# Cross attention and FP4 feed-forward on one core: two TensorE products taken from fp32 operands to pairs of fp16 parts, with one scale for the whole context of a batch element

## The reference, cut to what matters

```python
def xattn(inp_q, ctx, ctx, Wt, Wp, Wg, Wz, gamma, beta):      # inp_q = layernorm(x)
    t = einsum('oc,bcd->bod', Wt, ctx)
    p = einsum('oc,bcd->bod', Wp, inp_q)
    g = einsum('oc,bcd->bod', Wg, ctx)
    att = einsum('bgcd,bgcd->bg', pg, gg) * 0.125             # one score for each of 8 groups of 32 channels
    u = einsum('goc,bgcd->bgod', Wz, att * tg)
    xn = groupnorm(u) * gamma + beta
    return xn + ctx
x = x + xattn(layernorm(x), ctx, ctx, ...)
gate, up = fp4(layernorm(x)) @ fp4(w_gate).T, fp4(layernorm(x)) @ fp4(w_up).T
x = x + fp4(silu(gate) * up) @ fp4(w_down).T                  # 512 -> 1408 -> 512
```

## Time and profile before

| what | before |
|---|---|
| median of 3 runs | 1733.88 us (1733.24 to 1734.05) |
| the profiled execution | 1733.28 us, of which the span of the profile is 1731.4 us |
| TensorE matmuls busy | 1677.1 us, 97% of the span |
| VectorE busy | 1501.5 us, 87% |
| ScalarE busy | 825.9 us, 48% |
| GpSimd busy | 722.5 us, 42% |
| mean granted TensorE clock | 0.998 of full speed |

### The profile page before, as it was taken

The page is one execution under the profiler, slowest core; times in us unless marked ns, Lnnn a source line. Parts: engine busy times, 40 slices in busy tenths (PEclk is TensorE's granted clock), DMA queues, the critical chain, the costliest instruction groups (busy, mean ns, idle before and its releaser), DMA issues.

```text
span 1731.4 us, 27880 instructions
## 1 busy us (share of the span) xinstructions
PE 1677.1 (97%) x8723; PEld 922.2 (53%) x8723; DVE 1501.5 (87%) x2577; ACT 825.9 (48%) x1472; POOL 722.5 (42%) x951
## 2 busy tenths in 40 slices
PE   2799999999999999999999999999999999999999
PEld 1665555555555555555555555555555555555544
DVE  7877888889888888988888898888888988888887
ACT  3665544544445444444545444454544445445422
POOL 7986343334444333444433334443333444433310
PEclk9999999999999999999999999999999999999999
DMA  8123334343434344343334434333434444343322
GB/s 258 34 43 81 83 91 95 88 100 89 95 81 94 89 91 99 88 106 76 88 89 100 94 85 104 76 89 91 103 88 94 95 82 92 91 94 88 76 50 49
DMA packets 412150, 155.86 MB, mean 90 GB/s; under 512 B 383200, under 2 KB 384480, under 8 KB 412128
## 3 DMA queue, kind: packets, MB, share of 16 engines
q1 hardware_dynamic: 396352, 125.17, 33.9%
q10 hardware_dynamic: 15776, 30.41, 5.5%
HBM read 43.03 MB, written 16.78 MB: 35 GB/s over the span
## 4 chain that ended last, share of the span: by engine, by line
PE 91%; POOL 6%; DVE 1%; DMA 1%; issue 1%; ACT 0%; SPq 0%; POOLq 0%; DVEq 0%; ACTq 0%
PE pairs L550 52%; PE work L561 26%; PE work L500 5%; PE work L512 3%; PE work L527 2%; PE ubank L527 2%; POOL raw L1864 2%; POOL raw L1853 1%; POOL w_parts L1864 1%; POOL w_parts L1853 1%; DMA raw<-in_L_ffn_w_gate 0%; DMA hT_parts<-raw 0%; POOL xc L1787 0%; PE pairs L580 0%; POOL q_parts L1803 0%
## 5 line engine op out<-in xcount | busy, mean ns | idle before, releaser
L550 PE MATMUL pairs<-w_gate_hi,xT_parts 128*128 128x512 f16 (+1 forms) x1536 | 555.1, 361 | 0.5 <-DMA xT_parts<-raw 0.5
L550 PE MATMUL pairs<-w_up_hi,xT_parts 128*128 128x512 f16 (+1 forms) x1536 | 554.7, 361 | 0.0
L561 PE MATMUL work<-w_parts,hT_parts 128*128 128x512 f16 x2079 | 458.9, 379 | 0.9 <-DMA hT_parts<-raw 0.9
L561 PEld LDWEIGHTS work<-w_parts,hT_parts 128*128 128x128 f16 x2079 | 203.5, 99 | 236.0 <-issue 1.1
L550 PE MATMUL pairs<-w_up_lo,xT_parts 128*128 128x512 f16 (+1 forms) x768 | 277.5, 361 | 0.0
L550 PE MATMUL pairs<-w_gate_lo,xT_parts 128*128 128x512 f16 (+1 forms) x768 | 277.4, 361 | 0.0
L550 PEld LDWEIGHTS pairs<-w_gate_hi,xT_parts 128*128 128x128 f16 x1536 | 152.7, 99 | 155.7 <-issue 8.2
L550 PEld LDWEIGHTS pairs<-w_up_hi,xT_parts 128*128 128x128 f16 x1536 | 150.3, 98 | 146.8
L964 ACT ACTIVATE early<-pairs,w_unit 128x512 f32<-128x512 f32 (+1 forms) x192 | 124.8, 650 | 163.2 <-PE pairs L550 163.2
L915 ACT ACTIVATE wm<-h 128x1408 bf16<-128x1408 f32 (+2 forms) x65 | 87.2, 1341 | 204.9 <-DVE h L1184 204.9
L873 ACT CAST raw<-hq 128x704 f16<-128x704 f32 x126 | 98.2, 779 | 180.0 <-DVE hq L1201 179.3
(11 more groups left out here) (193 smaller groups left out, 2801.7 us busy)
## 6 DMA issues: line engine op xcount, KB each, us to landing
out<-raw SPq DMA_DIRECT2D x64, 256.0 KB, 2.1
c_in<-in_ctx ACTq DMA_DIRECT2D x29, 512.0 KB, 3.8
x_in<-in_x ACTq DMA_DIRECT2D x29, 512.0 KB, 5.2
raw<-in_L_ffn_w_down SPq DMA_DIRECT2D x2, 1408.0 KB, 8.8
raw<-in_L_ffn_w_gate SPq DMA_DIRECT2D x2, 1280.0 KB, 8.5
w_parts<-in_L_ffn_w_up SPq DMA_DIRECT2D x2, 1280.0 KB, 9.2
x_in<-in_x SPq DMA_DIRECT2D x3, 512.0 KB, 4.1
c_in<-in_ctx SPq DMA_DIRECT2D x3, 512.0 KB, 4.7
```

The costliest lines, as they stand in the source:

```text
L550: mm = pe.matmul(pairs[:, pair, n, 0:b - a], xT[s][part][:, k, :], w1[n][wpart][:, k, a:b], start=(k == 0 and part == 0 and wpart == 0), s ...
L561: mm = pe.matmul(obank[:, :], hT[part][:, k, :], w2[wpart][:, k, :], start=(k == 0 and part == 0 and wpart == 0), stop=(k == KH - 1 and pa ...
```

## The change

`mixed` and `u_rows` take pairs of fp16 parts. For that the context of an element gets one power-of-two scale for all its 256 rows in place of one for each row, so that the scale can be taken out after the products; both weight matrices get one scale each. The same scaled fp16 parts `c_parts` that `turn_c` turns are now read by `u_rows` as well.

- **TensorE.** `mixed` issues 12 fp16 matmuls of 256 columns in place of 4 fp32 ones; `u_rows` issues its 12 matmuls of 512 columns from fp16 parts. `mixed` waits for `gram_lo`.
- **ScalarE.** `gram_copy` is one instruction that writes the high fp16 part. `ctx_hi` and `ctx_fit_lo` go (4 instructions of a 128x512 tile). `ctx_fit` writes the fp16 part and the scaled fp32 context, 4 instructions, and now stands behind `affine(i+1,0)`. Two DMAs are issued: `save_rows` writes the 256 sums of squares to DRAM after `ctx_square`, and `spread_rows` reads them back to all partitions, behind `silu_group(j,0,0)` and ahead of `copy_u`.
- **VectorE.** New are `gram_lo` (one instruction of 128x512, behind `normalise2`), `ctx_peak` (a maximum over 256 numbers, behind `gated(j,0,1)`) and `scale_of_u` (2 numbers). `ctx_power` moves from ahead of `gated(j,0,0)` to behind `gated(j,0,2)`, with `scale_of_u` behind it.
- **GpSimd.** `ctx_root` waits for `ctx_peak` and stands behind `columns`. Both `ctx_lo` stand behind `columns_affine`; each subtracts the fp16 part from the scaled fp32 context and waits for both outputs of `ctx_fit` of its tile.
- **The opening.** For element 0 the maximum over the partitions goes over TensorE (`attention_peak`, `attention_rows`, `attention_top`, `attention_spread`, `attention_parts`), together with the maxima of the two weight matrices; `attention_hi` and `attention_lo` make their fp16 parts. Elements 1 and 2 use the DRAM path.

```diff
@@ tensor
             def mixed(b):
-                pe.wait_ge(gram_copied, HT * b + HT)
+                pe.wait_ge(gram_lo_done, b + 1)
                 at_least(pe, pg_summed, HT * b)
                 dst = mixed_bank(b)
                 for s in range(HT):
                     for k in range(HT):
-                        mm = pe.matmul(dst[:, s * C:(s + 1) * C], wgT[:, k, s * P:(s + 1) * P], gram_sb[:, k, :],
-                                       start=(k == 0), stop=(k == HT - 1))
+                        for wpart, part in PARTS:
+                            mm = pe.matmul(dst[:, s * C:(s + 1) * C], wgT[wpart][:, k, s * P:(s + 1) * P], gram_sb[part][:, k, :],
...
-                        mm = pe.matmul(u_bank(b, s), wuT[wpart][:, k, s * P:(s + 1) * P], c_wide[part][:, k, :],
+                        mm = pe.matmul(u_bank(b, s), wuT[wpart][:, k, s * P:(s + 1) * P], c_parts[:, k, part, :],
...
+            def attention_rows():
+                pe.wait_ge(wu_peaked, 2)
+                pe.wait_ge(c_squared, HT)
+                for n, column in enumerate((wu_pow[:, 0, 0:1], wu_pow[:, 0, 1:2], c_norm[:, 0, 0:1], c_norm[:, 0, 1:2])):
+                    mm = pe.matmul(mixed_bank(0)[0:1, n * P:(n + 1) * P], column, ident[:, :], start=True, stop=True)
...
@@ scalar
+            def save_rows(b):
+                act.wait_ge(c_squared, HT * b + HT)
+                at_least(act, c_rows_spread, 16 * (b - 1))
+                nc.scalar.dma_start(c_rows, c_norm[:, 0, :]).then_inc(c_rows_saved, 16)
+            def spread_rows(b):
+                act.wait_ge(c_rows_saved, 16 * b)
+                at_least(act, c_peaked, b)
+                nc.scalar.dma_start(c_all[:], c_rows.rearrange("p h -> (p h)").unsqueeze(0).to_broadcast([P, HT * P])
...
             def ctx_fit(b):
...
                 for s in range(HT):
                     nc.scalar.activation(c_parts[:, s, 0, :], c_in[:, s, :], ACT.Identity,
-                                         scale=c_norm[:, 2, s:s + 1]).then_inc(c_fit_done, 1)
+                                         scale=c_norm[:, 2, 0:1]).then_inc(c_fit_done, 1)
+                    nc.scalar.activation(c_scaled[:, s, :], c_in[:, s, :], ACT.Identity,
+                                         scale=c_norm[:, 2, 0:1]).then_inc(c_scaled_done, 1)
...
@@ scalar, body(i)
                 silu_group(j, 0, 0)
+                if ahead:
+                    spread_rows(i + 2)
                 if more:
                     copy_u(i + 1, 0)
                     copy_u(i + 1, 1)
...
+                silu_group(j, 0, 1)
+                x_hi(j + 1)
+                silu_group(j, 0, 2)
+                if more:
+                    affine(i + 1, 0)
                 if ahead:
                     ctx_fit(i + 2)
-                silu_group(j, 0, 1)
-                x_hi(j + 1)
-                if ahead:
-                    ctx_hi(i + 2)
-                silu_group(j, 0, 2)
-                if more:
-                    affine(i + 1, 0)
-                if ahead:
-                    ctx_fit_lo(i + 2)
                 grain_h(j)
@@ vector
+            def gram_lo(b):
+                dve.wait_ge(gram_copied, b + 1)
+                nc.vector.scalar_tensor_tensor(out=gram_sb[1][:].rearrange("p h n -> p (h n)"), in0=gram_bank(b)[:, 0:HT * C],
+                                               scalar=SS, in1=gram_sb[0][:].rearrange("p h n -> p (h n)"), op0=ALU.mult,
+                                               op1=ALU.subtract).then_inc(gram_lo_done, 1)
...
@@ vector, body(i)
                 normalise2(j + 1)
+                if more:
+                    gram_lo(i + 1)
                 h_snap_add(j - 1)
...
                     ln1_moments(i + 2, 0)
-                    ctx_power(i + 2)
                 gated(j, 0, 0)
...
                 gated(j, 0, 1)
                 if ahead:
+                    ctx_peak(i + 2)
                     ln1_moments(i + 2, 1)
...
                 gated(j, 0, 2)
+                if ahead:
+                    ctx_power(i + 2)
+                    scale_of_u(i + 2)
                 h_first(j)
@@ gpsimd
             def ctx_lo(b, s):
-                pool.wait_ge(c_hi_done, HT * b + s + 1)
-                nc.gpsimd.tensor_tensor(c_wide[1][:, s, :], c_in[:, s, :], c_wide[0][:, s, :].bitcast(F32),
-                                        ALU.subtract).then_inc(c_ready, 1)
+                pool.wait_ge(c_fit_done, HT * b + s + 1)
+                pool.wait_ge(c_scaled_done, HT * b + s + 1)
+                nc.gpsimd.tensor_tensor(c_parts[:, s, 1, :], c_scaled[:, s, :], c_parts[:, s, 0, :],
+                                        ALU.subtract).then_inc(c_fit_ready, 1)
...
@@ gpsimd, body(i)
+                columns(i + 1)
                 if ahead:
                     ctx_root(i + 2)
-                columns(i + 1)
+                columns_affine(i + 1)
                 if ahead:
                     ctx_lo(i + 2, 0)
-                columns_affine(i + 1)
-                if ahead:
                     ctx_lo(i + 2, 1)
                     add_ctx(i + 2, 0)
@@ the opening, vector
             normalise1(0, 0)
-            attention_lo()
+            attention_peak()
             weight_top(0)
+            attention_top()
             weight_max(1, 0)
             normalise1(0, 1)
             weight_unit(0)
+            ctx_peak(0)
+            weight_max(1, 1)
             ctx_power(0)
-            weight_max(1, 1)
+            attention_parts()
+            scale_of_u(0)
             weight_round(0)
+            attention_lo()
...
             copy_group(0)
+            ctx_peak(1)
             ctx_power(1)
```

More of the change, by code:

```diff
@@ L39 @@
 QS = 2.0 ** 10
+SS = 2.0 ** -10
 def at_least(eng, sem, n):
@@ L958, in weight_grain, with attention_hi @@
                 grain(wm[n % 2], staged(m, c * H, H), w_y_done, n + 1, w_grain_done)
+            def attention_hi():
+                act.wait_ge(wu_steps, 6)
+                for n, (full, parts) in enumerate(((wu_full, wuT), (wg_full, wgT))):
+                    nc.scalar.activation(parts[0][:, :, :].rearrange("p a b -> p (a b)"), full, ACT.Identity,
+                                         scale=wu_pow[:, 4, n:n + 1]).then_inc(wu_hi_done, 1)
             def silu_group(j, s, c):
@@ L993, in _ @@
             ctx_square(1)
+            save_rows(1)
             weights_lo(0)
             weights_lo(1)
+            spread_rows(1)
             weights_hi(2)
@@ L1088, in _ @@
             ctx_square(2)
+            save_rows(2)
             affine(1, 0)
+            spread_rows(2)
             weights_lo(31)
@@ L1120, in body @@
                     ctx_square(i + 2)
+                    save_rows(i + 2)
                 h_hi(j - 1, 0)
@@ L1130, in body @@
                     u_moments(i + 1, 1)
-                if ahead:
-                    ctx_fit(i + 2)
                 silu_group(j, 0, 1)
                 x_hi(j + 1)
-                if ahead:
-                    ctx_hi(i + 2)
                 silu_group(j, 0, 2)
@@ L1140, in body @@
                 if ahead:
-                    ctx_fit_lo(i + 2)
+                    ctx_fit(i + 2)
                 grain_h(j)
@@ L1474, in weight_round, with attention_peak @@
                                                op1=ALU.subtract).then_inc(w_r_done, 1)
-            def attention_lo():
-                dve.wait_ge(attw_copied, 3)
-                nc.vector.tensor_tensor(wuT[1][:, :, :].rearrange("p a b -> p (a b)"), pairs[:, 1, 0, :],
-                                        wuT[0][:, :, :].bitcast(F32).rearrange("p a b -> p (a b)"),
-                                        ALU.subtract).then_inc(attw_split, 1)
+            def attention_peak():
+                dve.wait_ge(attw_copied, 3)
+                for n, full in enumerate((wu_full, wg_full)):
+                    nc.vector.tensor_reduce(wu_pow[:, 0, n:n + 1], full, AX_X, ALU.max,
+                                            apply_absolute_value=True).then_inc(wu_peaked, 1)
@@ L1484, in _ @@
+            def attention_lo():
+                for n, (full, parts) in enumerate(((wu_full, wuT), (wg_full, wgT))):
+                    hi, lo = (parts[part][:, :, :].rearrange("p a b -> p (a b)") for part in range(2))
+                    dve.wait_ge(wu_hi_done, n + 1)
+                    nc.vector.scalar_tensor_tensor(out=lo, in0=full, scalar=wu_pow[:, 4, n:n + 1], in1=hi, op0=ALU.mult,
+                                                   op1=ALU.subtract).then_inc(attw_split, 1)
             ln1_moments(0, 0)
@@ L1507, in _ @@
             weight_round(3)
+            gram_lo(0)
             weight_scales(1, 1)
@@ L1517, in _ @@
             variance(0)
+            scale_of_u(1)
             ln1_moments(1, 1)
@@ L1563, in _ @@
             h_y(0)
+            gram_lo(1)
             weight_round(10)
@@ L1586, in _ @@
             h_lo(0, 0)
+            ctx_peak(2)
             ctx_power(2)
+            scale_of_u(2)
             x_scales(2)
```

140 lines of the change are left out of this document (92 added, 48 removed).

## The result

The changed kernel takes 1764.80 us, the median of 5 runs (1762.89 to 1765.86), against 1733.88 (1733.24 to 1734.15) of the kernel before: ratio 1.0178, 95% interval 1.0167 to 1.019, 31 us slower. The prediction had slower as the likeliest, with 1754.8; the result is 10 us above that and 0.8 us above the top of the range. The profiled execution has a span of 1764.1 us.

What follows compares the result with a forecast made beforehand. The prediction took TensorE, busy 97% of the span, to bound the kernel until something makes it wait. From the profiled 1733.3 us, +13.9 in the loop and +7.6 in the opening gave 1754.8, range 1718 to 1764.

Steps and rivals of the forecast that it cites:

- the sign: Whole kernel: slower than before, chance 0.55; faster had 0.35, same 0.10.
- the loop: The 30 bodies: 0.5 us more for each of 29, less 0.6 in the last, +13.9 us.
- TensorE in a body: TensorE's products in one body: 4.53 us removed, 3.90 added, so 0.63 us less if it never waits.
- Where the two `ctx_lo` land: GpSimd in the body: both block VectorE, `h_snap_add` is 1.6 us late, TensorE waits 1.15 in all.
- The margin: The last turned tile before TensorE's `output(j)` may be 0.45 us late before TensorE waits.
- The steps that I costed at nothing: In the loop: `gram_lo` on VectorE, `ctx_fit` leaving its old place on ScalarE, `save_rows` and `spread_rows`; no time lost.
- a meeting: Both `ctx_lo` collide with VectorE in the body: main case, chance 0.52, own range 1742 to 1768 us.
- ports shared in halves: SBUF ports shared by bandwidth, nothing blocked: the sum would be the first rival's, 1722.0 us, chance 0.31.
- the round trip through DRAM: Rival in the loop: `spread_rows` waits for `save_rows`; 1754 us without the `ctx_lo` collision, 1787 with it, chance 0.05.
- my two bounds: Landing time of `save_rows`: 2.1 us as for a 256 KB store, 5.2 as for a 512 KB load.
- the opening: Before the loop, hanging on GpSimd: +3.2, +2.2, +0.7 and +1.5, sum +7.6 us, bounds 3 and 10.
- the top of the range: Whole kernel: 1764 us, from a delay of 1.9 us in the loop with the full opening of 7.6.

Runs made afterwards that it cites:

- experiment 1: The changed kernel, but in the loop both `ctx_lo` subtract only 32 of the 512 columns: 1732.40 us.
- experiment 2: The changed kernel with the context of element i+2 prepared earlier in the body, no arithmetic changed: 1732.59 us.
- experiment 6: The kernel before the change, but in the loop its `ctx_lo(i+2,1)` runs three times in a row: 1752.44 us.
- after: The changed kernel itself, as profiled, against the kernel before: 1764.80 us, ratio 1.0178.
- experiment 3: The changed kernel, but in the loop `ctx_lo(i+2,1)` subtracts only 32 of 512 columns, `ctx_lo(i+2,0)` whole: 1740.90 us.
- experiment 4: The changed kernel, but in the loop `ctx_lo(i+2,0)` subtracts only 32 of 512 columns, `ctx_lo(i+2,1)` whole: 1737.25 us.
- experiment 5: The changed kernel, but in the loop each `ctx_lo` runs twice into the same tile: 1864.50 us.
- experiment 7: The changed kernel with `gram_lo(0)` and `gram_lo(1)` earlier on VectorE in the opening: 1756.09 us.
- experiment 8: The changed kernel with the opening's `ctx_root(1)` behind `columns(0)` on GpSimd, and `ctx_power(1)` and `scale_of_u(1)` behind `variance(0)` on VectorE: 1759.05 us.

## Why the prediction was right and wrong

**Right: the sign, and the loop to 0.1 us.** Forecast +13.9 us from the first `gram` of the loop to the end, by a period of 50.72; measured 50.71 and 32.7 - 18.8 = +13.9. That the sums meet to the tenth is chance: the prediction rounded 0.52 a body to 0.5, and unrounded it would have had +14.5. Each step holds. *TensorE in a body*: 3.90 forecast, 3.89 in the chain, and 49.56 as soon as nothing waits (experiments 1 and 2). *Where the two `ctx_lo` land*: `h_unit` +0.85 forecast, +0.94 measured; `residual` +1.0, +0.96; waits 0.8 and 1.15 in all, 0.84 by the starts and 1.15 (50.71 - 49.56) measured. *The margin* of 0.45 at `output(j)` comes out as 0.4 in experiment 6. The steps that I costed at nothing, `gram_lo` in the loop, `ctx_fit` off its old place, `save_rows` and `spread_rows`, cost nothing that these runs can tell. The rule of the Trainium skill (SBUF — State Buffer, who interferes with whom) is that VectorE, with two SBUF inputs or in a two-port mode, and a GpSimd instruction that reads SBUF exclude each other, and the second to issue is blocked until the first is finished. The traces agree: in five kernels with a meeting (after and experiments 3 to 6) 0.27 becomes 1.2, 0.7 becomes 1.6 and 1.6 becomes 2.6 or 2.7, each by about what was left of the GpSimd instruction, and in the two without one (experiments 1 and 2) none of these grows by more than 0.05. By an estimate from its own 0.27 us, ports shared in halves would have made `h_unit` 0.27 longer, not 0.94.

**Right by luck: the round trip through DRAM.** I took 2.1 us for `save_rows`, the price of a store of 256 KB. The view of tile `c_rows` has

```profile
DMA to landing us min/median/max: 2.6/3.5/4.4
```

At the median that is 1.4 us more than I took, for 1 KB, and between my two bounds. The save is issued at 803.85, so the spread can be issued at 807.4 at the median, and it is wanted at 807.6 (the forecast's 782.8, moved to this body); TensorE's `group_means` waited for ScalarE in no body of the loop of after. The one late body each in experiments 3 and 4 shows how near it is.

**Wrong: the opening, +7.6 forecast, +18.8 measured.** The step that failed is "`ctx_root(1)` stood at 57.76, and its new releaser is queued behind `copy_group(0)` at 59.48, a row and 0.5 later: +2.2". `ctx_root(1)` came 11.2 late, of which 4.2 are those of `ctx_root(0)`: 7.0 in place of 2.2. The step took `copy_group(0)` at its time in the old trace. Its own input had got a new instruction in front: `gram_copy`, `gram_lo(0)`, `mixed(0)`, `u_rows`, `group_means(0)`. I had checked `gram_lo` against its neighbours in the loop and priced `gram_lo(1)` at its own 0.7 us, but never asked behind what `gram_lo(0)` and `gram_lo(1)` are queued on VectorE: an instruction of 0.7 us made `mixed` wait 4.4 and 3.6, and TensorE ran at half its clock behind each wait. Step by step, the starts in the two traces give: `ctx_root(0)` +4.2 (forecast 3.2); from there to `ctx_root(1)` +7.0 (2.2); to `gram(1)` +3.4 (nothing forecast; on the way GpSimd idles 2.4 us for ScalarE and 3.9 for VectorE, and before it did not); to `mixed(1)` +3.8 (0.7 for `gram_lo(1)`); to the first `gram` of the loop +0.4 (1.5 for `ctx_power(2)`). Moving the two saves 8.7 us (experiment 7), letting `weight_y(5)` past the wait 5.7 more (8). Of the remaining 4 to 5, `ctx_root(0)` was forecast +3.2 and came +4.2, since the maxima over TensorE had to wait for `c_squared` until 22.0 (L647). The upper bound of 10 for the opening is that sum with 2.4 on top, for which the prediction gives no working. And the top of the range, 1764, took 7.6 for the opening and a delay of 1.9 in the loop, although the meeting's own range went to 1768.

## What to carry to other kernels

An instruction added to a busy in-order queue costs its consumer the queue ahead of it, not its own length; look that up at every place where it is issued, prologue included, and follow moved releasers through the new times, not the old. Two engines that lock each other out of SBUF make the place of a GpSimd instruction as important as its length: put it beside instructions of VectorE that the trace shows unblocked, even when that means preparing data earlier. Here those were instructions with an operand in PSUM, row statistics and a maximum over one tile; one input tile alone is no safe sign, for `h_unit` and `h_scale` read one and were blocked (1.21 for 0.27, 0.88 for 0.19). Losses behind a margin don't add: one `ctx_lo` in the way cost 5 to 9 us by the medians (7 to 8 by the periods), two cost 32, four 132 (some 50 of them by the clock).

## What the runs showed of the hardware beyond that

- Blocking goes both ways and takes no account of size: GpSimd's 128x2 instruction `ln_rs` (L1895) took 1.52 us in the changed kernel, from 829.16 on, beside VectorE's `h_snap_back` (829.00, 1.62 us), and 0.20 in experiment 2, where it met the row statistics.
- TensorE's granted clock stayed at 1.00 behind the waits of 0.7 us in each body of the changed kernel, and was at half for about 3 us behind the waits of 3.0 us in experiment 5, where the wait cost 1.7 us more than itself.
